# Feed-forward halves of two batch elements alternating beside the distances, with buffers of their own, and layer norm applied on DVE

## What is computed

```
x = x + attn_a(layernorm(x))   # one distance matrix per element, shared by all 16 heads
x = x + ffn(layernorm(x))
x = x + attn_b(layernorm(x))   # 16 heads of 16 channels, causal
x = x + ffn(layernorm(x))      # the same weights again

attn_a: V = x wv^T + bv; pos = x w3d^T + b3d (3 numbers a token)
        attn = softmax over keys <= query of -|pos_q - pos_k| / 4;  out = (attn V) wo^T + bo
attn_b: k, q, v = x Wkqv + bkqv;  softmax of the causal q.k / 4, times v
ffn:    xp = x of the token before (0 for the first)
        r = sigmoid((mu_r x + (1-mu_r) xp) W_r^T);  k = (mu_k x + (1-mu_k) xp) W_k^T
        out = r * (relu(k)^2 W_v^T)
```

## Time and profile before

| | us |
|---|---|
| median of 3 runs | 2153.86 (2149.85 to 2161.84) |
| the profiled execution | 2155.86 |
| its span, first to last instruction | 2154.1 |
| PE, DVE, ACT, POOL busy in it | 1852.8, 1427.4, 1245.4, 1027.3 |
| mean granted TensorE clock | 0.941 of full speed |

### The profile page before, as it was taken

One profiled execution on the slowest core, in us unless ns is written; L12 is line 12 of the kernel. 1 busy time (PEld: TensorE's weight loads), 2 busy tenths in 40 slices (PEclk: granted clock), 3 DMA queues, 4 the chain that ended last, 5 costly groups with the idle time before them and its releaser, 6 DMA issues. The chain is left out here.

```text
span 2154.1 us, 32514 instructions
## 1 busy us (share of the span) xinstructions
PE 1852.8 (86%) x9842; PEld 921.0 (43%) x9842; DVE 1427.4 (66%) x4173; ACT 1245.4 (58%) x2673; POOL 1027.3 (48%) x1074
## 2 busy tenths in 40 slices
PE   4476799889998899988998899978998899988986
PEld 3344344434543355434544345424554345323423
DVE  2235767766786677776776676776876677777732
ACT  0722655685648655595557755495557756465562
POOL 4364254436662465435753366534753357314314
PEclk8778699999999999999999999999999999999988
DMA  3006010211223111311123111311123102322000
GB/s 103 1 8 140 1 31 23 67 30 30 40 88 60 31 30 55 74 31 30 41 74 74 30 21 49 89 31 30 31 77 79 24 11 40 98 47 44 1 21 20
DMA packets 64348, 97.27 MB, mean 45 GB/s; under 512 B 15656, under 2 KB 58030, under 8 KB 58031
## 3 DMA queue, kind: packets, MB, share of 16 engines
q1 hardware_dynamic: 64174, 95.20, 20.1%
HBM read 61.09 MB, written 33.55 MB: 44 GB/s over the span
## 5 line engine op out<-in xcount | busy, mean ns | idle before, releaser
L852 ACT ACTIVATE pt<-exp_bank 128x512 f32<-128x512 f32 (+3 forms) x1536 | 748.2, 496 | 664.7 <-PE exp_bank L822 657.5
L867 DVE CUSTOM_DVE_ANT_0 max_bank<-max_bank,mask 128x128 f32<-128x128 f32 (+3 forms) x1024 | 501.4, 501 | 402.1 <-PE max_bank L811 387.7
L811 PE MATMUL max_bank<-ks,qs 96*128 96x512 bf16 (+3 forms) x1536 | 517.9, 342 | 81.4 <-DVE piece_max L870 45.0
L822 PE MATMUL exp_bank<-qs,ks 98*128 98x512 bf16 (+3 forms) x1536 | 512.6, 340 | 69.2 <-ACT pt L852 67.0
L870 DVE TENSOR_REDUCE piece_max<-max_bank 128x1 f32<-128x512 f32 x512 | 343.5, 685 | 105.6 <-PE max_bank L811 102.3
L837 PE MATMUL o_bank<-pt,v 128*17 128x512 f32 (+3 forms) x3072 | 335.6, 510 | 7.6 <-ACT pt L852 3.1
L353 POOL TENSOR_SCALAR xh<-xs,mv,rstd 128x256 f32<-128x256 f32 x256 | 321.2, 1261 | 10.0 <-PE side L379 3.8
L811 PEld LDWEIGHTS max_bank<-ks,qs 96*128 96x128 bf16 x1536 | 150.6, 98 | 382.7 <-DVE piece_max L870 136.5
L889 POOL TENSOR_SCALAR_AFFINE_SELECT pt<-pt 128x512 f32<-128x512 f32 x256 | 170.4, 666 | 291.6 <-ACT pt L852 291.3
L822 PEld LDWEIGHTS exp_bank<-qs,ks 98*128 98x128 bf16 x1536 | 151.9, 100 | 281.4 <-ACT pt L852 174.6
L505 POOL TENSOR_TENSOR sq<-sq 128x512 f32<-128x512 f32 (+1 forms) x96 | 95.9, 999 | 230.1 <-ACT sq L451 230.1
(11 more groups left out here) (94 smaller groups left out, 2284.0 us busy)
## 6 DMA issues: line engine op xcount, KB each, us to landing
parts_dram<-parts SPq DMA_DIRECT2D x64, 384.0 KB, 2.6
qs<-parts_dram SPq DMA_DIRECT2D x192, 128.0 KB, 7.1
ks<-parts_dram SPq DMA_DIRECT2D x32, 384.0 KB, 4.7
xs<-in_L_attn_a_x_dram SPq DMA_DIRECT2D x16, 512.0 KB, 4.2
ks<-parts_dram SPq DMA_DIRECT2D x32, 256.0 KB, 5.4
out_dram<-xs SPq DMA_DIRECT2D x16, 512.0 KB, 3.0
ks<-parts_dram SPq DMA_DIRECT2D x32, 128.0 KB, 5.9
qs<-neg_maxT SPq DMA_DIRECT2D x64, 8.0 KB, 1.9
```

Of the source, the lines that this page charges most:

```text
L811: pe.matmul(max_bank[u % MAX_BANKS][:, 0:k1 - k0], qs[r][0:KROWS, j, P * tile:P * (tile + 1)], ks[r][0:KROWS, j, k0:k1], start=True, stop= ...
L822: pe.matmul(exp_bank[k % EXP_BANKS][:, 0:q1 - q0], ks[r][:, j, P * kt:P * (kt + 1)], qs[r][:, j, q0:q1], start=True, stop=True).then_inc(s ...
L852: act.activation(pt[:, e % 2, j, 0:q1 - q0], exp_bank[k % EXP_BANKS][:, 0:q1 - q0], ACT.Exp, scale=SCALE).then_inc(exp_done, 1)
L867: dve.tensor_tensor_reduce(scores, scores, mask[:, HALF - w:HALF], 1.0, LOWEST, ALU.add, ALU.max, piece_max[:, j, m:m + 1]).then_inc(max_f ...
```

## The change

It does five things.

1. The stages' halves are placed singly (`STARTS`, from the turn's first quarter): att1 -36 and -24, ffn4 38 and 74, ffn2 56 and 92, proj3 108 and 138. So the halves of ffn4 (element n-2) and ffn2 (element n) alternate every 18 quarters, while the distances (now from -4 to 76) and the attend parts still run. Element 0 has the same pattern shifted by `HEAD` = -200, and element 1 has no starts of its own.
2. The distance pieces get 4 to 8 quarters by width, 80 in all, from quarter 32; att1's values come every second quarter, the positions of the first half ahead of the second half's values, and the projections at `PROJECT_AT`. Lateness is regained at a third instead of a quarter.
3. `xk`, `xr`, `ka` and `th` are buffers of their own. The relu goes into `ka`, which is squared in place, and the product with r is written over `th`; `kr` and `tm` go. As two elements' halves now alternate in `xt`, the last column of a first half is kept in `edge` and put back ahead of the second half (two small ACT copies a stage).
4. To make room, `x32` and `parts` of proj3 become views of `p1`, with waits of both users for one another, and `ot` has one buffer instead of two.
5. The norm is applied by DVE instead of POOL, at the same quarters 7 to 10; DVE waits there for POOL's rstd. The functions of att1 are split in separate ones for values, positions, distances and residuals, so that each is put in order by its own quarter.

```
-ATT1, FFN2, FFN4, PROJ3 = -44, 50, 82, 114
-FIRST = {("att1", 0): -220, ("ffn2", 0): -126, ("proj3", 0): -74,
-         ("att1", 1): -28, ("ffn2", 1): 66, ("proj3", 1): 114}
+STARTS = {("att1", 0): -36, ("att1", 1): -24, ("ffn4", 0): 38, ("ffn2", 0): 56, ("ffn4", 1): 74, ("ffn2", 1): 92,
+          ("proj3", 0): 108, ("proj3", 1): 138}
+HEAD = -200
-LN_HALF = {"att1": 8, "ffn2": 16, "ffn4": 16, "proj3": 12}
...
-PIECE_TIME = [2 + (q1 - q0) // P for _, q0, q1 in KEY_PIECES] + [5, 5, 5]
-PIECE_AT = [34 + sum(PIECE_TIME[:p]) for p in range(NP + 4)]
+PIECE_TIME = [{P: 4, 2 * P: 5, 3 * P: 7, 4 * P: 8}[q1 - q0] for _, q0, q1 in KEY_PIECES] + [5, 5, 5]
+PIECE_AT = [32 + sum(PIECE_TIME[:p]) for p in range(NP + 4)]
...
+PROJECT_AT = [18, 22, 26, 30, 46, 49, 52, 55]
+VALUES_AT = [34, 37, 57, 59]
-        "att1": [("values1", t, 16 + t + TPH * (t // TPH), 1, 1, 2) for t in range(NT)] +
-                [("positions", k, 29 + k, 1, 1, 1) for k in range(6)] +
+        "att1": [("values1", t, 16 + 2 * t + TPH * (t // TPH), 1, 1, 2) for t in range(NT)] +
+                [("positions", k, 25 + k + 9 * (k // 3), 1, 1, 1) for k in range(6)] +
...
-        xr, xk, ka = (pb[:, k, :].rearrange("p (c n) -> p c n", c=NC) for k in range(3))
-        kr = sq[:, 0, 0:2, :]
-        th = sq[:, 1, 0:2, :].rearrange("p a (b c) -> p (a b) c", c=C)
-        tm = sb("tm", [P, TPH, C])
-        x32 = sb("x32", [P, 2, HALF])
-        parts = sb("parts", [P, 2, 3, HALF], BF16)
+        xk, xr, ka = (sb(name, [P, NC, HALF]) for name in ("xk", "xr", "ka"))
+        th = sb("th", [P, TPH, C])
+        edge = sb("edge", [P, 2, NC, 1])
+        x32 = p1[:, 0:2 * HALF].rearrange("p (r n) -> p r n", r=2)
+        parts = p1[:, 2 * HALF:5 * HALF].bitcast(BF16).rearrange("p (r k n) -> p r k n", r=2, k=3)
...
@@ dve_statistics
+            for t in range(TPH):
+                yield at(7 + t)
+                if t == 0:
+                    dve.wait_ge(rstd_ready, q + 1)
+                    if q > 0:
+                        dve.wait_ge(tr_full, 2 * q)
+                dve.tensor_scalar(xh[:, t, :], src[:, TPH * h + t, :], mv[:, r, t, 0:1], rstd[:, r, t:t + 1],
+                                  ALU.subtract, ALU.mult).then_inc(xh_ready, 1)
@@ pool_normalise
-            pool.wait_ge(rstd_ready, q + 1)
...
-                pool.tensor_scalar(xh[:, t, :], src[:, TPH * h + t, :], mv[:, r, t, 0:1], rstd[:, r, t:t + 1],
-                                   ALU.subtract, ALU.mult).then_inc(xh_ready, 1)
...
@@ act_transposed
+                    if h == 1 and s in ("ffn2", "ffn4"):
+                        act.wait_ge(edge_kept, EDGE_AT[s, n] + 1)
+                        act.activation(last, kept, ACT.Copy).then_inc(edge_put, 1)
...
@@ square
-                    if p == 0 and halves_before("att1", n, 0):
-                        act.wait_ge(tm_ready, 2 * halves_before("att1", n, 0))
@@ transform, first piece
+                        for r in range(2):
+                            act.wait_ge(part_stored[r], 64 * n)
@@ pool_ffn
-                    if s == "ffn2":
-                        pool.wait_ge(p1_exp, NP * (n + 1))
+                    if h == 1:
+                        pool.wait_ge(edge_put, EDGE_AT[s, n] + 1)
@@ act_proj3
+                if j == 0:
+                    act.wait_ge(pv1_full, 8 * (n + 1))
```

More of the change, by code:

```diff
@@ L1 @@
+import math
 from contextlib import ExitStack
@@ L347, in pool_normalise @@
             pool.tensor_tensor(rstd[:, r, :], var_eps[:, r, :], minus_half[:, :], ALU.pow).then_inc(rstd_ready, 1)
[L348 to L354 removed]
         def act_transposed(at, s, n, h):
             act, q = nc.scalar, LN_AT[s, n, h]
+            last = xt[:, :, XO + HALF - 1:XO + HALF]
+            kept = edge[:, 0 if s == "ffn2" else 1, :, :]
             for c in range(NC):
@@ L370, in act_transposed @@
                                ACT.Copy).then_inc(xt_ready, 1)
+            if h == 0 and s in ("ffn2", "ffn4"):
+                act.wait_ge(xt_ready, 2 * q + 2)
+                act.activation(kept, last, ACT.Copy).then_inc(edge_kept, 1)
         def pe_transposed(s, n, h):
@@ L381, in pe_transposed, with dve_values1 @@
                 mm.then_inc(tr_full, 1)
-        def dve_att1(at, n):
+        def dve_values1(n):
             dve = nc.vector
-            def values(t):
+            for t in range(NT):
+                yield EMPTIED_AT["values1", "att1", n, 0, t]
                 dve.wait_ge(v1_full, 8 * n + t + 1)
@@ L407, in distance, with dve_residuals @@
                                          op0=ALU.max, op1=ALU.add).then_inc(dist2_ready, 1)
-            def residual(t):
+        def dve_residuals(n):
+            dve = nc.vector
+            for t in range(NT):
+                yield EMPTIED_AT["attend", "att1", n, 0, t]
                 bank = side_of("attend", "att1", n, 0, t)
@@ L518, in values, with pe_positions @@
                 mm.then_inc(v1_full, 1)
-            def positions(c, h):
+        def pe_positions(n):
+            pe = nc.tensor
+            for k in range(6):
+                h, c = divmod(k, 3)
+                job = "positions", "att1", n, 0, k
+                yield PARTS_AT[job][0]
                 pe.wait_ge(vp_ready, 8 * n + TPH * (h + 1))
-                bank = side_job(("positions", "att1", n, 0, 3 * h + c), pb_ready, 6 * n + 3 * h + c + 1)
+                bank = side_job(job, pb_ready, 6 * n + k + 1)
                 for t in range(TPH):
@@ L527, in positions, with pe_attend @@
                 mm.then_inc(pb_full, 1)
+        def pe_attend(n):
+            pe = nc.tensor
             for t in range(NT):
-                yield PARTS_AT["values1", "att1", n, 0, t][0]
-                values(t)
-            for k in range(6):
-                yield PARTS_AT["positions", "att1", n, 0, k][0]
-                positions(k % 3, k // 3)
-            for t in range(NT):
-                yield PARTS_AT["attend", "att1", n, 0, t][0]
+                job = "attend", "att1", n, 0, t
+                yield PARTS_AT[job][0]
                 m = t + 1 if t < TPH else TPH + t + 1
```

155 lines of the change are left out of this document (71 added, 84 removed).

## The result

The changed kernel takes 2208.02 us (median of 4 runs, 2204.21 to 2211.06) against 2153.38 for the kernel before on the same chip: a ratio of 1.0247 [1.0211, 1.0283]. It is slower, and the forecast of 2072 had the sign wrong.

What follows compares the result with a forecast made beforehand. PE's idle time was taken as all a change could win. Head -31, first turn -3, six turns -45, last turn -1 and tail -4 gave -84: 2155.9 to 2072 us, own range 2040 to 2105, 8 in 10 2030 to 2135.

Steps and rivals of the forecast that it cites:

- What bounds the kernel now: Whole kernel: a change can win only PE's idle time, 23.8 us a turn at most, and the head.
- Distances over 80 quarters: First 48 quarters of a turn: about 46 us instead of 52.4; 6 us taken, between 0 and 10.4.
- rival A: Only the head wins; in the turns DVE's extra takes what the distances gave: 2121 us, chance 0.19.
- Halves at 38, 56, 74, 92: Second and fourth parts of a turn: feed-forward halves with own buffers win 2 and 1.5 us of idle time.
- Norm to DVE: Per turn, 32 instructions at 0.45 us (anchors about 0.25 to 0.28, and 0.418): 14.4 us of DVE, 2 on the path.
- A new wait on DVE: DVE waits at quarter 7 for POOL's rstd: 0 to 1 us lost eight times a turn, within the 2 us.
- Other edits: Edge copies, x32 and parts inside p1, th and ka in place: nothing on the path, waits met.
- Head, -31: Before the first attention matmul: a shorter chain of dependences starts attention near 171 us; -31, ends -15 and -45.
- Step (a): Head: first distances need only the first half's positions, so ACT's squares start near 50.5 instead of 58.38; -6.
- Step (b): Head: first halves of ffn2 and proj3 no longer wait for the second; last projection at 151, 25 us earlier.
- Tail: Last half's layer norm on DVE instead of POOL, rstd still waiting: -4 us, ends -2 and -6.
- C: Rival: slower, engines meet in DVE's queue; 2236 us with none hidden, 2180 half hidden; chance 0.12.

Runs made afterwards that it cites:

- pace 60: Changed kernel (norm on DVE) with the distance pieces at the old 60 quarters instead of 80, everything else new: 2181.21 us, 1.01 [1.0068, 1.0132].
- pace 72: Changed kernel with the distance pieces at 72 quarters (7, 6, 5, 4 by width) instead of 80: 2227.03 us, 1.0302 [1.027, 1.0334].

## Why the prediction was wrong

Against the forecast's parts the profiles give: head -9.4 us for -31, first turn +3.7 for -3, the six full turns +63.5 for -45, last turn -1.8 for -1, tail -7.4 for -4. So 108 of the 132 us between forecast and result lie in the full turns, and three terms of the sum failed there: the distances, the places of the halves and the norm's price on the path.

*What bounds the kernel now.* The reading held: PE idles 23 us a turn, 10.4 of them where ACT is at 94%. What it left out is that PE's idle time is no fixed stock from which edits only draw. "DVE and ACT have room over the whole turn" was an average. DVE had 28% free, and in the two kernels that added work to it, 55 to 60% of that work became time.

*Distances over 80 quarters, "I take 6 us".* ACT's wait fell by 8.3 us a turn, more than the 6 taken, but by luck: only 3.7 of it go with the pace (4.8 us at pace 60), the rest with the other edits, and no time was won by it. The first part took 51.2 us and not the 46 of the forecast: it has 1.1 us more of PE's work, and while the wait for ACT in it fell from 6.0 to 0.7, that for DVE grew to 5.1 and that of the side matmuls to 1.8. The rest came back in the second part, where the last distances, the attends and the first half of ffn4 now share quarters. At pace 60 this part is 5.3 us shorter and idles a third as much. The term had the wrong sign, -6 a turn, where the profiles of the two paces differ by +1.4 a turn, +11.5 in the sixth and +4.3 in the first (and -4.1 in the head). That is the text of rival A ("DVE's extra takes what the distances gave") at a larger price.

*Halves at 38, 56, 74, 92, "2 us and 1.5 us".* Instead of closing a gap, the alternation put the statistics and norm of one half on the mixes and product of others. PE's idle time rose by 0.4, 4.7 and 3.5 us in the last three parts. That this meeting of steps is what costs there is read from the timeline; no run parts it from the rest. With the norm on POOL the new places and pace cost 5.7%, 123 us, over the old order (1.0576 to 1.0003); with the norm on DVE 1.7%, 36 us (1.0247 to 1.0078), of which 32 come with the pace. So by themselves the alternating places were worth about nothing on DVE, and not -3.5 us a turn.

*Norm to DVE, "0.30 + 0.15 us" and "on the path I count 2 us a turn".* The instruction's median is 0.406 us, near bn_stats over the same columns (0.418), the upper of my two anchors; its mean of 0.498 is 0.05 over the 0.45 of the sum. This size is a small error: 15.9 us of DVE a turn for 14.4. The path is the large one. "The second bank covers most" failed: 7.9 us a turn at the old places instead of 2, over half of the added time, of which 4.0 are idle time and 3.9 the longer busy time of PE that the sum had nowhere. My account of it, argued and not shown by a run of its own: two banks can take up one delay, but not 0.41 to 1.12 us in each of four quarters running beside a row maximum of 0.6 to 0.7 in a quarter of 1.3.

*A new wait on DVE.* Right: 0.8 us a turn for rstd, inside the 0 to 1 us per norm at its lower end. Whole run 18.4 us: 5.1 in the head, 6.9 in the tail and the rest in the turns.

*Other edits, at nothing.* Right: 1.0003 [0.9988, 1.0018] with all of them and the old order. Not named there were the inner offsets, which the change also moves by a quarter. They cost nothing in the changed kernel, and 70 us in the old places.

*Head, -31.* Step (a) was right (squares at 51.24, forecast 50.5). Step (b) failed. Its terms as they stand add up to 155 us for the last projection and not to 151; above all, the chain through proj3's second half was counted as one norm and four projections, but its statistics queue behind the first half's casts on DVE, and its transposes come at 154.57 where the sum had the last projection at 151. Norm on DVE alone gives -12 to -13 in the old order, so the new order contributed nothing to the head, or took 3 us. Tail: -7.4 for -4, beyond my -6; 2.8 of it are PE's busy time at a granted clock of 0.85 for 0.79, which the norm's move can't claim.

*The clock.* The forecast counted only idle time. PE's busy time per turn rose by 3.8 us on average on the same instructions, with a granted clock of 0.94 to 0.97 in the five turns for 0.97 to 0.98. In the kernel with the norm on POOL, where PE idles 32 us a turn, the clock is 0.94 and PE is busy 230.6 us. So a part of each turn's loss is slower matmuls. It doesn't follow PE's idle time alone: at pace 72 PE idles 33.5 us in a turn and is busy 225.9, at 0.97.

*The rivals.* C named the place ("DVE's queue becomes the place where all engines meet"), and its two figures, 2180 with half hidden and 2236 with nothing hidden, lie 28 us to either side of the result. It got 0.12, because I argued that POOL would lose just those instructions that DVE waits for. POOL's additions, squares and differences remained, and the alternation set them beside DVE's mixes. The range's upper end, 2135, stopped short of C, although nothing in the trace showed a DVE with more work in the ring. The row that should have warned was in the table of waits: DVE at 72% already cost 7.1 us a turn of first-pass waits, and the prediction uses that view for the first part only.

*Left open.* Why pace 60 is better than 80 and 72, the largest single piece of the loss: carried lateness is refuted, the peak of lateness isn't parted from the pace, and DVE's overlap with POOL isn't measured separately. Nor is it shown how the loss divides between the places of att1 and proj3 and those of the feed-forwards.

## What to carry to other kernels

The cost of moved work isn't its duration on an engine with idle time: it depends on what stands behind it in that engine's queue. Where DVE empties a ring of two banks, 55 to 60% of what was added to it became time at a busy share of 72 to 77% (taking half of the norm off again won nothing, as POOL then had it), while outside the ring the same move won 12.9 us in the head and 3.6 in the tail. So split such a move by stretch before splitting it by kind of work. And before spreading or interleaving stages, write down quarter by quarter which steps of two neighbours meet on the same engine, and what in-order work waits behind a step that can stall.

## What the runs showed of the hardware

- One quarter, about 1.3 us, in the issue of a POOL difference together with one in the receptance matmul costs 70 us over the kernel (1.0328 against 1.0003). A stalled instruction holds the masks queued behind it, and PE's waits for these grow by 38 us; the rest isn't traced.
- A DVE mix of 0.75 us takes up to 1.86, and a norm instruction of 0.41 up to 1.37, when POOL works on SBUF at the same time. bn_stats over the same columns never does: 0.42 us on average beside POOL as without it, 0.43 at most. At 256 columns with two per-partition scalars tensor_scalar isn't faster than bn_stats (0.406, 0.418).
- PE's busy time on the same matmuls of a turn lies between 222 and 235 us, with the granted clock from 0.98 down to 0.92. In the kernel before it is 222.4 us on average, with 23.4 us idle, at 0.97 to 0.98. Idle time alone doesn't fix it: 230.5 at 32.6, at 0.94 (norm on POOL), 225.9 at 33.5, at 0.97 (pace 72).
